# Four-layer graph network: when the second layer turns its attention weights, adds its elu and takes the next moments

## The chip, the core and the metric

The kernel runs on one core of a Trainium2 chip. The metric is the device time of one execution in microseconds, 724.43 as the median of three. The engines are TensorE (PE, with its weight loads listed as PEld), VectorE (DVE), ScalarE (ACT), GpSimd (POOL) and SyncE (SP). Each runs its own list of instructions in order; between engines, semaphores are counted up (`then_inc`) and waited for (`wait_ge`).

## What is computed

64 graphs of 128 nodes and 256 features pass four layers. Each layer normalises, applies relu, computes and adds its result to x:

```python
h = jnp.maximum(_layernorm(x), 0.0); x = x + L0(h)   # relations
h = jnp.maximum(_layernorm(x), 0.0); x = x + L1(h)   # attention with leaky relu, below
h = jnp.maximum(_layernorm(x), 0.0); x = x + L2(h)   # normalised adjacency
h = jnp.maximum(_layernorm(x), 0.0); x = x + L3(h)   # attention with 8 heads

# L1, the second layer
h = jnp.einsum('bnc,cf->bnf', x, W)
s1 = jnp.einsum('bnf,f->bn', h, a1); s2 = jnp.einsum('bnf,f->bn', h, a2)
e = jax.nn.leaky_relu(s1[:, :, None] + s2[:, None, :], negative_slope=0.2) * mask
att = jax.nn.softmax(e, axis=2)
out = jax.nn.elu(jnp.einsum('bij,bjf->bif', att, h) + beta * h)
```

## The kernel before

x stays in SBUF for all layers (`xs`). The work goes by pairs of graphs, 32 of them (`PAIRS`), and a layer is a software pipeline over the pairs: in step p each engine works on several pairs, each at a different stage. Everything is written out in Python; the order on each engine is the order of the code.

In step p of the second layer **PE** runs `product(p)` (L385, the features times W), `turn_prob(p - 3)` (L848, transposes the attention weights of pair p - 3 into bank 3), `turn(p + 1)` (L166, transposes the next normalised input), `attend(p - 3)` (L835, weights attT times values) and `spread(p)` (L873, one score as a row). The banks for attend are three, so attend(q) waits until elu(q - 3) has read its bank (`l1_x_done`).

**ACT** runs `copy_pT(p - 3)` (L912, the turned weights to attT), `copy_h(p)` (L907), `copy_hT(p + 1)` (L916), `softmax_exp(p - 1)` (L922), and for elu of pair p - 4 `elu_negative` (L929) and `elu_exp` (L935). `normalise_early(q)` (L282) are the first inputs of the third layer; number 0 stands after step 29, the others behind the loop.

**DVE** runs `scores(p - 1)` in step p: masked (L1019), inverse, leaky (L1026), `attention(p - 2)` (L1041, the weights), `elu(p - 6)` (L853, adds the positive part from the bank to x), maximum (L1031). Behind it stand the moments of odd pairs of this layer (L361, one graph in an odd step; in an even step the other, and then L366, L143 and L144 for nmean and vare), and in 16 steps, `UNIT_STEPS`, half a unit of the third layer's first moments (`moments_two`: L252, and at every second half L257). They are steps 8 to 26 without 12, 17 and 22. Behind the units of pairs 3 and 7 follow the arguments for the roots (L263, L264).

**POOL** in step p: every other step a root for an odd pair (L155), in steps 22 and 28 `root_two` (L270, L272, eight roots of the third layer); then it waits until attention(p - 2) is done, runs `add(p - 5)` (L987, the exponential part of elu onto x) and `centre_first(p + 2)` (L331, the normalised input). `add_bias_two` (L307) belongs to the third layer.

Behind the loop, the **tail** mixes the last pairs of the second layer with the first of the third: `gather` (L375), `outputs` (L395), `gathered_high` (L290) and `gathered_low` (L295), `update_two` (L301).

Of the kernel before, what the change touches and what calls it, by code (L numbers as in the profile page):

```python
# [9 lines left out]
ALU = mybir.AluOpType  # L10
# [4 lines left out]
def gnn_stack_kernel(nc, x, adj, w):  # L15
# [3 lines left out]
    PAIRS = GRAPHS // 2  # L19
# [10 lines left out]
    with ExitStack() as ctx:  # L30
# [215 lines left out]
        def moments_two(dve, q, g):  # L246
# [6 lines left out]
            if g == 1:  # L253
                ins.then_inc(l2_step, 1)
                dve.wait_ge(l2_step, 2 * q + 1)
                for g in range(2):
                    ins = nc.vector.bn_aggr(mv_two[:, q, g, :], stats_two[:, g, :])  # L257
                ins.then_inc(l2_step, 1)
                if q % 4 == 3:
                    dve.wait_ge(l2_step, 2 * q + 2)  # L260
                    mean, var = (mv_two[:, q - 3:q + 1, :, i].rearrange("p k g -> p (k g)") for i in range(2))
                    part = slice(2 * q - 6, 2 * q + 2)
                    nc.vector.scalar_tensor_tensor(nmean_two[:, part], mean, -2.0, mean, ALU.mult, ALU.add)  # L263
                    nc.vector.scalar_tensor_tensor(vare_two[:, part], var, EPS, var, ALU.add, ALU.max).then_inc(l2_two_stats, 1)  # L264
# [164 lines left out]
        with nc.Block() as block:  # L429
# [427 lines left out]
            def _(pe):  # L857
# [19 lines left out]
                def step(p):  # L877
                    product(p)
                    if p >= 3:
                        turn_prob(p - 3)  # L880
# [6 lines left out]
                    spread(p)  # L887

# [11 lines left out]
                turn_prob(PAIRS - 3)  # L900

            @block.scalar
            def _(act):
# [32 lines left out]

                def step(p):
# [7 lines left out]
                    if p >= 4:  # L945
                        elu_negative(p - 4)
                        elu_exp(p - 4)

                def elu_parts(p):
                    elu_negative(p)  # L950
                    elu_exp(p)
# [13 lines left out]
                elu_parts(PAIRS - 5)  # L965
# [18 lines left out]
            def _(pool):  # L984
# [4 lines left out]
                for p in range(PAIRS):  # L989
# [8 lines left out]
                    if p >= 5:  # L998
                        add(p - 5)
                    if p + 2 < PAIRS:  # L1000
                        centre_first(pool, p + 2, tr_done, p + 1)
                for p in range(3):
                    add_bias_two(pool, p)
                add(PAIRS - 5)
                add_bias_two(pool, 3)
# [8 lines left out]
            def _(dve):  # L1014
# [30 lines left out]
                def scores(p):  # L1045
# [6 lines left out]
                    if p >= 5:  # L1052
                        elu(p - 5)
                    maximum(p)

                def step(p):
# [9 lines left out]
                    if p in UNIT_STEPS:  # L1066
                        unit = UNIT_STEPS.index(p)
                        moments_two(dve, unit // 2, unit % 2)

                UNIT_STEPS = [p for p in range(8, 27) if p % 5 != 2]  # L1070
# [7 lines left out]
                elu(PAIRS - 6)  # L1078
# [4 lines left out]
                elu(PAIRS - 5)  # L1083
# [552 lines left out]
```

## Time and profile before

| | before |
|---|---|
| median of 3 runs | 724.43 us (724.25 to 724.78) |
| the profiled execution | 724.73 us, span 722.7 us |
| PE busy | 699.0 us (97%) |
| DVE busy | 623.9 us (86%) |
| ACT busy | 554.1 us (77%) |
| POOL busy | 461.7 us (64%) |
| chain of waits: PE, DVE, ACT | 87%, 6%, 3% |

The profile is of one execution; its time stands beside the span of its instructions. Starts are counted from the span's start. A row of the timeline gives start, duration, engine and line of the source, what is written and read, and in brackets how long the engine had been idle and who released it. The modelled end of a PE row reaches into the next, so PE is read by starts. The second layer's loop lies between about 180 and 300 us. PE's granted clock is 1.00 in every stretch of it.

### The profile page before, as it was taken

To read this page: it belongs to the slowest core of one execution; us is meant where nothing else is said; L and a number is where in the kernel's file an instruction comes from. 1 tells how busy PE (TensorE), PEld (TensorE's weight loads), DVE (VectorE), ACT (ScalarE), POOL (GpSimd) and SP (SyncE) were. 2 spreads that over 40 slices of the span, in tenths; PEclk is the share of its full clock that TensorE was granted. 3 is DMA by queue.
4 is the path that set the end of the run, shared out by engine and by line. 5 is a ranking of instruction groups with operands and counts; after the bars stand their busy time and mean duration, and the time that the engine had idled before them with its cause. 6 is when DMAs were issued, how large, how long until landed. Compare 5 with 4: busy or idle time off the path is not lost.

```text
span 722.7 us, 22547 instructions
## 1 busy us (share of the span) xinstructions
PE 699.0 (97%) x6938; PEld 655.3 (91%) x6938; DVE 623.9 (86%) x2618; ACT 554.1 (77%) x1892; POOL 461.7 (64%) x585
## 2 busy tenths in 40 slices
PE   6999999999999999999998999999999999999996
PEld 5999999998788787889998899999999999999995
DVE  5898988886789998689998998989988998988865
ACT  3666565655688888976664988899888988898895
POOL 2455545464477677678884767766677667766762
PEclk9999999999999999999999999999999999999999
DMA  7223300000000000000000000000000000000001
GB/s 243 84 84 98 88 29 0 0 0 1 0 1 2 1 2 0 2 1 1 0 0 1 17 18 31 29 29 15 29 29 29 27 18 29 29 29 16 31 32 44
DMA packets 21710, 20.30 MB, mean 28 GB/s; under 512 B 2449, under 2 KB 21649, under 8 KB 21649
## 3 DMA queue, kind: packets, MB, share of 16 engines
q1 hardware_dynamic: 19456, 18.16, 8.0%
q10 hardware_dynamic: 2192, 1.44, 0.7%
q8 instruction: 24, 0.39, 0.2%
q14 instruction: 38, 0.30, 0.2%
HBM read 11.21 MB, written 8.39 MB: 27 GB/s over the span
## 4 chain that ended last, share of the span: by engine, by line
PE 87%; DVE 6%; ACT 3%; issue 2%; DMA 1%; POOL 0%; ACTq 0%; DVEq 0%
PE bank L395 43%; PE bank L1278 8%; PE bank L385 5%; PE bank L166 5%; PE bank L1264 5%; PE bank L1288 4%; PE bank L478 4%; PE bank L835 4%; PE bank L425 3%; PE bank L375 3%; DVE xs L853 1%; PE bank L459 1%; DVE att L1041 1%; ACT prob L1374 1%; PE bank L873 1%
## 5 line engine op out<-in xcount | busy, mean ns | idle before, releaser
L1374 ACT ACTIVATE prob<-wide,small 128x128 f32<-128x128 f32 x504 | 195.7, 396 | 2.1 <-DVE small L1486 2.1
L1449 POOL TENSOR_TENSOR prob<-prob,small 128x512 f32<-128x512 f32 x127 | 132.2, 1042 | 100.1 <-DVE small L1500 98.1
L1486 DVE CUSTOM_DVE_ANT_0 wide<-bank,mbias 128x128 f32<-128x128 f32 x512 | 115.2, 285 | 0.1
L1374 ACT ACTIVATION_READ_ACCUMULATOR prob<-wide,small 128x1 f32 x504 | 97.9, 194 | 0.0
L155 POOL TENSOR_TENSOR rstd<-vare,mhalf 128x2 f32<-128x2 f32 x104 | 73.6, 708 | 19.8 <-DVE vare L144 19.6
L1278 PE MATMUL bank<-ident,prob 128*128 128x128 f32 x512 | 72.8, 275 | 3.5 <-POOL prob L1449 3.2
L634 POOL TENSOR_TENSOR rnorm<-norm,mhalf 128x2 f32<-128x2 f32 x32 | 22.3, 695 | 81.3 <-ACT relsq L575 81.3
L129 DVE BATCH_NORM_STATS2 stats<-xs 128x6 f32<-128x256 f32 (+1 forms) x176 | 65.5, 413 | 5.4 <-DMA xs<-in_x_dram 4.5
L239 POOL TENSOR_SCALAR xn<-xs,nmean,rstd 128x256 f32<-128x256 f32 x120 | 65.4, 554 | 5.5 <-POOL rstd L155 5.5
L1394 ACT COPY probT<-bank 128x512 f32<-128x512 f32 x96 | 52.4, 580 | 19.6 <-PE bank L1278 19.6
L1278 PEld LDWEIGHTS bank<-ident,prob 128*128 128x128 f32 x512 | 59.0, 141 | 4.9 <-POOL prob L1449 4.8
L385 PE MATMUL bank<-w,hT 128*128 128x258 f32 x256 | 61.4, 382 | 1.3 <-DVE oTs L741 1.1
L987 POOL TENSOR_TENSOR xs<-xs,exp_u 128x512 f32<-128x512 f32 x32 | 40.8, 1276 | 30.2 <-DVE att L1041 28.0
L166 PE MATMUL bank<-ident,xn 128*128 128x128 f32 x376 | 56.4, 272 | 0.0
L395 PE MATMUL bank<-w,yTs 128*128 128x256 f32 x384 | 53.4, 288 | 2.2 <-DVE xs L301 2.1
L395 PE MATMUL bank<-hTs,wq 128*128 128x256 f32 x384 | 54.3, 290 | 0.6 <-DVE hTs L1504 0.6
L395 PE MATMUL bank<-hTs,wk 128*128 128x256 f32 x384 | 53.7, 288 | 0.0
L395 PE MATMUL bank<-wv,hTs 128*128 128x256 f32 x384 | 53.5, 288 | 0.0
L385 PEld LDWEIGHTS bank<-w,hT 128*128 128x128 f32 x256 | 46.1, 190 | 7.4 <-issue 1.3
L395 PE MATMUL bank<-wo,oTs 128*128 128x256 f32 x384 | 51.4, 284 | 1.0 <-DVE oTs L1538 0.5
L395 PEld LDWEIGHTS bank<-hTs,wq 128*128 128x128 f32 x384 | 47.6, 188 | 4.4 <-DVE hTs L1504 0.8
L395 PEld LDWEIGHTS bank<-w,yTs 128*128 128x128 f32 x384 | 47.5, 189 | 4.4 <-DVE yTs L295 2.4
(168 smaller groups left out, 1930.9 us busy)
## 6 DMA issues: line engine op xcount, KB each, us to landing
out_dram<-xs SPq DMA_DIRECT2D x31, 256.0 KB, 2.1
xs<-in_x_dram SPq DMA_DIRECT2D x29, 256.0 KB, 2.7
xs<-in_x_dram ACTq DMA_DIRECT2D x1, 512.0 KB, 7.2
xs<-in_x_dram ACTq DMA_DIRECT2D x1, 256.0 KB, 3.8
wq<-in_L_gnn_Wq_dram SPq DMA_DIRECT2D x1, 256.0 KB, 3.4
wk<-in_L_gnn_Wk_dram ACTq DMA_DIRECT2D x1, 256.0 KB, 4.7
wv<-in_L_gnn_Wv_dram SPq DMA_DIRECT2D x1, 256.0 KB, 5.3
w<-in_L_gnn_W_dram SPq DMA_DIRECT2D x1, 256.0 KB, 7.0
```

Source lines behind the costliest of these rows:

```text
L129: ins = nc.vector.bn_stats(stats[:, b, g, :], x_of(p, g))
L155: nc.gpsimd.tensor_tensor(rstd[:, b, :], vare[:, b, :], mhalf[:, 0:2], ALU.pow).then_inc(rstd_ready, 1)
L166: ins = nc.tensor.transpose(pe_ps[:, c * 2 * N + g * N:c * 2 * N + (g + 1) * N], src[:, g, c * 128:(c + 1) * 128], ident[:, :])
L239: ins = nc.gpsimd.tensor_scalar(xnb[b][:, g, :], x_of(p, g), nmean[:, b, g:g + 1], rstd[:, b, g:g + 1], ALU.add, ALU.mult)
L385: ins = nc.tensor.matmul(ps_g, hT[:, c, g, :], weight[:, c, :], start=(c == 0), stop=(c == C - 1))
L395: ins = nc.tensor.matmul(ps, lhsT(a, c), rhs(b, c), start=(n == 0), stop=(n == len(terms) - 1))
L987: nc.gpsimd.tensor_tensor(x_pair(p), x_pair(p), exp_u[p % 2][:, :, :], ALU.add).then_inc(added, 1)
L1278: ins = nc.tensor.transpose(PT[r % 2][:, i * N:(i + 1) * N], prob[:, r, i, :], ident[:, :])
L1374: ins = nc.scalar.activation(prob[:, r, i, :], wide[:, r, i, :], ACT.Exp, bias=nmax[r][:, i:i + 1], scale=-1.0, accum_out=rsum[r][:, i:i + 1])
L1394: nc.scalar.copy(prob_turned[b][r], PT[r % 2][:, :].rearrange("p (i n) -> p i n", n=N)).then_inc(pt_ready, 1)
L1449: nc.gpsimd.tensor_tensor(prob[:, r, :, :], prob[:, r, :, :], rinv[r].unsqueeze(2).to_broadcast([128, QUAD, N]), ALU.mult).then_inc(prob_r ...
L1486: nc.vector.tensor_tensor_reduce(out=wide[:, r, i, :], in0=SS[r][:, i * N:(i + 1) * N], in1=mbias[:, :], scale=-1.0, scalar=3e38, op0=ALU. ...
```

## The change

The turn of a pair's attention weights moves to the end of the step in which DVE makes them: `turn_prob(p - 2)` as PE's last operation of step p, instead of `turn_prob(p - 3)` behind the product. Elu moves up by one step on ACT (pair p - 3 in step p), POOL (`add(p - 4)`) and DVE (`elu(p - 5)` in step p). The tail loses the pieces that moved into the loop. The third layer's moments stand in steps 8 to 15 and 18 to 25, and the arguments of the roots are an own function, in steps 17 and 27.

```diff
+        def root_arguments_two(dve, k):
+            dve.wait_ge(l2_step, 8 * k + 8)
+            mean, var = (mv_two[:, 4 * k:4 * k + 4, :, i].rearrange("p k g -> p (k g)") for i in range(2))
+            part = slice(8 * k, 8 * k + 8)
+            nc.vector.scalar_tensor_tensor(nmean_two[:, part], mean, -2.0, mean, ALU.mult, ALU.add)
+            nc.vector.scalar_tensor_tensor(vare_two[:, part], var, EPS, var, ALU.add, ALU.max).then_inc(l2_two_stats, 1)
...
                 def step(p):
                     product(p)
-                    if p >= 3:
-                        turn_prob(p - 3)
                     if p + 1 < PAIRS:
                         turn(p + 1)
...
                     if p >= 3:
                         attend(p - 3)
                     spread(p)
+                    if p >= 2:
+                        turn_prob(p - 2)
...
                 gather_nodes(pe, bank[1], 1, xn2, l2_xn_ready).then_inc(l2_yt_done, 1)
-                turn_prob(PAIRS - 3)
...
                     if p >= 1:
                         softmax_exp(p - 1)
-                    if p >= 4:
-                        elu_negative(p - 4)
-                        elu_exp(p - 4)
+                    if p >= 3:
+                        elu_parts(p - 3)
...
                 normalise_early(act, 2)
-                elu_parts(PAIRS - 5)
                 softmax_exp(PAIRS - 1)
...
-                    if p >= 5:
-                        add(p - 5)
+                    if p >= 4:
+                        add(p - 4)
...
-                    if p >= 5:
-                        elu(p - 5)
+                    if p >= 4:
+                        elu(p - 4)
...
+                    elif p in (17, 27):
+                        root_arguments_two(dve, p // 10 - 1)
-                UNIT_STEPS = [p for p in range(8, 27) if p % 5 != 2]
+                UNIT_STEPS = [*range(8, 16), *range(18, 26)]
```

PE, steps 30 and 31 and the end of the loop, before (`att0` and `att1` are the two buffers of the weights, `val` the values, `nadjT` the adjacency for the third layer):

```order
L385 MATMUL bank<-w1,hT 128x258 x4
L848 MATMUL bank<-ident,att1 128x128 x2
L166 MATMUL bank<-ident,xn2 128x128 x4
L835 MATMUL bank<-val3,attT 128x256 x2
L873 MATMUL bank<-ident,val2 128x128 x2
L385 MATMUL bank<-w1,hT 128x258 x4
L848 MATMUL bank<-ident,att0 128x128 x2
L375 MATMUL bank<-nadjT,xn 128x128 x4
L835 MATMUL bank<-val0,attT 128x256 x2
L873 MATMUL bank<-ident,val3 128x128 x2
L375 MATMUL bank<-nadjT,xn2 128x128 x4
L848 MATMUL bank<-ident,att1 128x128 x2
```

The same place after (its lines are numbered higher by two):

```order
L387 MATMUL bank<-w1,hT 128x258 x4
L166 MATMUL bank<-ident,xn2 128x128 x4
L837 MATMUL bank<-val3,attT 128x256 x2
L875 MATMUL bank<-ident,val2 128x128 x2
L850 MATMUL bank<-ident,att0 128x128 x2
L387 MATMUL bank<-w1,hT 128x258 x4
L377 MATMUL bank<-nadjT,xn 128x128 x4
L837 MATMUL bank<-val0,attT 128x256 x2
L875 MATMUL bank<-ident,val3 128x128 x2
L850 MATMUL bank<-ident,att1 128x128 x2
L377 MATMUL bank<-nadjT,xn2 128x128 x4
```

The turn of `att0`, which stood between the product and attend of step 31, now ends step 30, and that of `att1` ends step 31 ahead of the second gather.

ACT behind the loop, before (`xn2`, `xn`: early normalisations 1 and 2; `yTs`: gathered, high part):

```order
L907 COPY val3<-bank 128x516
L282 ACTIVATE xn2<-xs,shift_two,rstd_two 128x256 x2
L290 CAST yTs00<-bank 128x512
L922 ACTIVATE exp_e0,small<-leaky_e0,small 128x128 x2
L912 COPY attT<-bank 128x256
L290 CAST yTs10<-bank 128x512
L282 ACTIVATE xn<-xs,shift_two,rstd_two 128x256 x2
L929 ACTIVATE neg_u<-bank 128x512
L935 ACTIVATE exp_u1<-neg_u 128x512
L922 ACTIVATE exp_e1,small<-leaky_e1,small 128x128 x2
```

And after:

```order
L908 COPY val3<-bank 128x516
L284 ACTIVATE xn2<-xs,shift_two,rstd_two 128x256 x2
L292 CAST yTs00<-bank 128x512
L923 ACTIVATE exp_e0,small<-leaky_e0,small 128x128 x2
L913 COPY attT<-bank 128x256
L292 CAST yTs10<-bank 128x512
L284 ACTIVATE xn<-xs,shift_two,rstd_two 128x256 x2
L923 ACTIVATE exp_e1,small<-leaky_e1,small 128x128 x2
L913 COPY attT<-bank 128x256
```

The two elu operations ahead of the last pair's exponentials are gone from here.

DVE in step 14, before, from the weights of pair 12 on:

```order
L1041 SCALAR_TENSOR_TENSOR att0<-exp_e0,small,beta_ident 128x128 x2
L853 SCALAR_TENSOR_TENSOR xs<-bank,xs 128x512
L1031 TENSOR_REDUCE small<-leaky_e1 128x2
L361 BN_STATS stats<-xs 128x6
L366 BN_AGGR mv<-stats 128x2 x2
L143 SCALAR_TENSOR_TENSOR nmean<-mv 128x2
L144 SCALAR_TENSOR_TENSOR vare<-mv 128x2
L252 BN_STATS stats_two<-xs 128x6
L257 BN_AGGR mv_two<-stats_two 128x2 x2
```

In step 13, after, from the weights of pair 11 on:

```order
L1038 SCALAR_TENSOR_TENSOR att1<-exp_e1,small,beta_ident 128x128 x2
L855 SCALAR_TENSOR_TENSOR xs<-bank,xs 128x512
L1028 TENSOR_REDUCE small<-leaky_e0 128x2
L363 BN_STATS stats<-xs 128x6
L252 BN_STATS stats_two<-xs 128x6
L257 BN_AGGR mv_two<-stats_two 128x2 x2
```

Before, the heavier half of a unit came now in an even step, behind the longer half of the odd moments, now in an odd one; after, it always stands in an odd step.

## Rows read from the trace of the kernel before

**Rows 1.** Timeline: PE in steps 3 and 31; start, duration (us), engine, line, operation.

```profile
187.84 1.61 PEld L385 LDWEIGHTS bank<-w,hT 128*128 128x128 f32 x8 [0.31 <-ACT hT L916]
...
295.61 1.91 PE L385 MATMUL bank<-w,hT 128*128 128x258 f32 x8
```

**Rows 2.** Busy time by engine in five steps of the second layer.

```profile
245.60:264.50 18.90, 18.78 (x101) 15.40 (x101) 17.74 (x65) 15.68 (x44) 14.50 (x19) 1.00 0.00 1
```

**Rows 3.** Timeline: one step's PE operations, with two of ACT's in it.

```profile
249.20 1.91 PE L385 MATMUL bank<-w,hT 128*128 128x258 f32 x8
...
250.95 0.38 PE L848 MATMUL bank<-ident,att 128*128 128x128 f32 x2
...
251.17 0.60 PE L166 MATMUL bank<-ident,xn 128*128 128x128 f32 x4
...
251.37 0.37 ACT L912 COPY attT<-bank 128x256 f32<-128x256 f32 x1 [0.51 <-PE bank L848]
...
251.79 0.73 PEld L835 LDWEIGHTS bank<-val,attT 128*128 128x128 f32 x4 [0.26 <-ACT attT L912]
...
252.76 0.38 PE L873 MATMUL bank<-ident,val 128*128 128x128 f32 x2
...
252.98 1.91 PE L385 MATMUL bank<-w,hT 128*128 128x258 f32 x8
...
253.38 0.60 ACT L929 ACTIVATE neg_u<-bank 128x512 f32<-128x512 f32 x1
```

**Rows 4.** Table of waits: who waited for whom, us in total, times, longest.

```profile
PEld bank L835 <- ACT attT L912: 9.3, 28, 0.8
...
PE bank L835 <- DVE xs L853: 1.9, 5, 0.6
```

**Rows 5.** Timeline: PE, an attend whose weights were ready, and what follows.

```profile
298.47 1.03 PE L835 MATMUL bank<-val,attT 128*128 128x256 f32 x4
...
299.34 0.38 PE L873 MATMUL bank<-ident,val 128*128 128x128 f32 x2
```

**Rows 6.** Timeline: DVE, the end of one step and the steps before and after 249.45.

```profile
233.28 0.41 DVE L252 BATCH_NORM_STATS2 stats_two<-xs 128x6 f32<-128x256 f32 x1
...
233.89 0.58 DVE L1019 SCALAR_TENSOR_TENSOR masked_e<-bank,val,adj_sb 128x128 f32<-128x128 f32 x2
...
245.63 0.61 DVE L1019 SCALAR_TENSOR_TENSOR masked_e<-bank,val,adj_sb 128x128 f32<-128x128 f32 x2 [0.85 <-PE bank L873]
...
249.45 0.59 DVE L1019 SCALAR_TENSOR_TENSOR masked_e<-bank,val,adj_sb 128x128 f32<-128x128 f32 x2
...
250.07 0.42 DVE L1026 SCALAR_TENSOR_TENSOR leaky_e<-masked_e 128x256 f32<-128x256 f32 x1
...
251.87 0.42 DVE L361 BATCH_NORM_STATS2 stats<-xs 128x6 f32<-128x256 f32 x1
...
252.20 0.41 DVE L252 BATCH_NORM_STATS2 stats_two<-xs 128x6 f32<-128x256 f32 x1
```

**Rows 7.** Timeline: POOL's add and centre in that step, and its early root.

```profile
251.10 1.27 POOL L987 TENSOR_TENSOR xs<-xs,exp_u 128x512 f32<-128x512 f32 x1 [0.78 <-DVE att L1041]
...
252.36 1.10 POOL L331 TENSOR_SCALAR xn<-xs,nmean,rstd 128x256 f32<-128x256 f32 x2
...
260.97 1.65 POOL L270 TENSOR_TENSOR rstd_two<-vare_two,mhalf 128x8 f32<-128x8 f32 x1
```

**Rows 8.** Timeline: one operation of POOL and one of DVE in the tail.

```profile
316.86 1.28 POOL L987 TENSOR_TENSOR xs<-xs,exp_u 128x512 f32<-128x512 f32 x1 [1.32 <-ACT exp_u L935]
...
317.00 1.16 DVE L143 SCALAR_TENSOR_TENSOR nmean<-mv 128x2 f32<-128x2 f32 x1
```

**Rows 9.** Timeline: PE's product of step 30, ACT's early normalisation.

```profile
291.48 1.91 PE L385 MATMUL bank<-w,hT 128*128 128x258 f32 x8
...
293.04 1.08 ACT L282 ACTIVATE xn<-xs,shift_two,rstd_two 128x256 f32<-128x256 f32 x2
```

**Rows 10.** Timeline: PE, the outputs of pair 7 in the third layer.

```profile
323.58 1.68 PE L395 MATMUL bank<-w,yTs 128*128 128x256 f32 x12
```

More of the change, by code:

```diff
@@ L258, in moments_two @@
                 ins.then_inc(l2_step, 1)
[L259 to L264, printed above, removed]
+        def root_arguments_two(dve, k):
[4 more added lines that the diff above has]
+            nc.vector.scalar_tensor_tensor(vare_two[:, part], var, EPS, var, ALU.add, ALU.max).then_inc(l2_two_stats, 1)
         def root_two(pool, k):
@@ L935, in elu_exp, with elu_parts @@
                     nc.scalar.activation(exp_u[p % 2][:, :, :], neg_u[:, :, :], ACT.Exp, scale=-1.0).then_inc(eu_ready, 1)
+                def elu_parts(p):
+                    elu_negative(p)
+                    elu_exp(p)
                 def step(p):
@@ L944, in step @@
                         softmax_exp(p - 1)
-                    if p >= 4:
-                        elu_negative(p - 4)
-                        elu_exp(p - 4)
-                def elu_parts(p):
-                    elu_negative(p)
-                    elu_exp(p)
+                    if p >= 3:
+                        elu_parts(p - 3)
                 for p in range(PAIRS - 1):
@@ L997, in _ @@
                         pool.wait_ge(prob_ready, p - 1)
-                    if p >= 5:
-                        add(p - 5)
+                    if p >= 4:
+                        add(p - 4)
                     if p + 2 < PAIRS:
                         centre_first(pool, p + 2, tr_done, p + 1)
-                for p in range(3):
+                for p in range(4):
                     add_bias_two(pool, p)
-                add(PAIRS - 5)
-                add_bias_two(pool, 3)
                 add(PAIRS - 4)
@@ L1077, in _ @@
                 attention(PAIRS - 2)
-                elu(PAIRS - 6)
+                elu(PAIRS - 5)
                 maximum(PAIRS - 1)
@@ L1082, in _ @@
                 attention(PAIRS - 1)
-                elu(PAIRS - 5)
                 update_two(dve, 0, 0)
```

## The prediction

> **What bounds the kernel now.** I read the busy time by stretches first, then the step starts in the timeline, then the table of waits, then single steps on each engine. TensorE (PE) is busy nearly throughout, so a change can pay only where PE waits or where one of its instructions takes longer than it must. The second layer is such a place. Its step p = 3 begins at 187.84 and its step 31 at 295.61 [rows 1]: 107.77 us for 28 steps, 3.85 each. In five steps without disturbance (245.60 to 264.50) each engine has, per step of 3.78: PE 3.76, VectorE (DVE) 3.55, ScalarE (ACT) 3.14, GpSimd (POOL) 2.90 [rows 2]. PE looks full there, but it isn't at its own rate. One step reads, by starts [rows 3]: product 249.20 to 250.95 (1.75), turn of the weights to 251.17 (0.22), turn of the next input, whose four transposes are twice two and so 0.44, attend at 251.79, spread at 252.76, next product at 252.98 (0.22). Attend's weight load stood idle for 0.26 until ACT had copied attT. The table of waits has this 28 times, 9.3 us in all, and beside it 1.9 us in which attend waited for elu on DVE (xs L853) [rows 4]. An attend whose attT was there long before takes 0.87 from its start to the next instruction [rows 5]. So a step without a wait costs 1.75 + 0.22 + 0.44 + 0.87 + 0.22 = 3.50 us, and PE now pays 3.78 and more.
>
> **The turn of the weights.** It moves from behind the product of step q + 3 to the end of step q + 2. Between it and attend(q) lay the 0.44 us of one turn, in which ACT had to see it, copy it (it begins at 251.37, after an idle 0.51 [rows 3]) and tell PE; now the product lies there as well, 2.19 us in all. What it waits for is attention(q), which DVE ends about 1.6 us into step q + 2, while its new place is 3.28 into that step: no wait until DVE is 1.6 late. The number of instructions is unchanged. Removed per step: 3.78 - 3.50 = 0.28, the 0.26 of the weight load [rows 3] and rounding. The product, now right behind it, waits for hT; ACT no longer sits waiting for the turned weights before it copies val and hT, so it makes hT earlier, and I cost this at nothing.
>
> **Elu one step up.** attend(q) needs elu(q - 3) done, for the bank. That elu was in the same step's DVE work, just before attend; it is now one step earlier, so the 1.9 us of [rows 4] go. ACT's two elu operations for p - 3 now wait for an attend of the same step; attend ends about 3.2 into the step, ACT came to the first of them at 253.38, 4.18 after the product's start, and comes the 0.5 us earlier in which it sat idle before attT [rows 3], so at about 3.7. POOL's add(p - 4) needs the exponential of the step before, which ends about 1.4 into the step; POOL starts the add at 1.65, released by attention [rows 6, 7]. Both are nothing while these covers of 0.5 and 0.3 us last, and each costs what exceeds them. ACT's own work, 3.14 per step, leaves 0.36 of 3.50.
>
> **What is late next: DVE with POOL.** The moments of the third layer now lie in steps 8 to 15 and 18 to 25 with no gap. An even step of that kind holds the full odd moments and half a unit: 249.45 - 245.63 = 3.82. An odd one holds 251.87 - 249.45 = 2.42 for the scores and elu, 252.20 - 251.87 = 0.33 for half of the odd moments, and 233.89 - 233.28 = 0.61 for the heavy half of a unit: 3.36 [rows 6]. Steps without a unit are 0.33 shorter at even p (3.49) and take 2.75 at odd p; the root arguments that now stand in steps 17 and 27 (two small operations) fall into such short steps. But DVE can't always go as fast as that. POOL's add holds DVE's nmean: begun at 317.00 under an add that began at 316.86 and lasts 1.28, it takes 1.16 instead of 0.15 to 0.3, and ends 0.02 after the add [rows 8]. leaky and attention read two SBUF operands like it. In the loop of before nothing of POOL lies on them, since the add waits for attention, and add and centre are over 252.36 + 1.10 - 249.45 = 4.01 us after DVE began the step, while the next leaky comes 0.62 into the following one [rows 6, 7]. At a shorter period they touch: a DVE step is then not under 4.01 - 0.62 = 3.39. The Trainium skill, page "SBUF — State Buffer", section "Who interferes with whom", says that a DVE instruction with two SBUF inputs and a GpSimd instruction that reads SBUF exclude each other for a whole instruction, the later one blocking; the stretched nmean agrees, and by that rule the same floor follows. If the row stood only for nmean's own small form and leaky and attention ran freely, the floor would fall away, and the demand below would be 1.5 less.
>
> DVE's demand from step 8 to 27 is then 8 x (3.82 + 3.39) + 2 x (3.49 + 3.39) = 71.4 us against PE's 20 x 3.50 = 70.0: 1.4 late. POOL's root for eight values, 1.65 [rows 7] and with the shift behind it about 1.89, stays in steps 22 and 28 and pushes the end of add and centre to 0.62 + 1.89 + 1.26 + 1.10 = 4.87; leaky is then held by 4.87 - (3.82 + 0.62) = 0.4 and, in the shorter step 28, by 4.87 - (3.49 + 0.62) = 0.8. That makes 2.6 us late in all. How late may DVE be before PE waits? The maximum comes 2.42 into a DVE step; behind it ACT runs exponentials, two elu operations and the copy of attT, some 2.2 us (3.14 less about 0.95 for the copies of val and hT, an estimate), and attend needs this at 3.50 + 2.19 = 5.69. That is about 1.0 us of room, so PE loses 2.6 - 1.0 = 1.6. The bounds: nothing, if lag is absorbed or the floor isn't there; and 4.4, if POOL's later operations hold leaky for another 0.28 (a quarter of centre's 1.10) in each of these ten odd steps. I take 1.6, since the 3.82 and 3.36 are measured and only the room is an estimate.
>
> **Step 30.** ACT's first early normalisation (293.04, two of them 1.08 long [rows 9]) lies between two steps; it made step 30 last 295.61 - 291.48 = 4.13 [rows 1, 9]. It adds about 1.03 to ACT's 3.14 and now meets a shorter period: 3.14 + 1.03 - 3.50 = 0.67, so step 30 is 4.17. What was won by the early turn is given back in this one step.
>
> **The tail** runs from step 31 to the product of pair 7 in the third layer at 323.58 [rows 10], 27.97 us. ACT loses one pair's two elu operations there, each about as long as the 0.60 of [rows 3], so the exponentials of pair 31 can come some 1.1 earlier. But ACT later waits again for the turn of pair 31, whose place in PE's order is unchanged, and PE comes to it only as much earlier as its own waits shrink: attend(29) no longer waits for elu (0.25), and the low half for pair 0 is 0.2 earlier. I take 0.5; bounds 0 and 1.1. POOL's lock on nmean at 317.00 can shift either way, 0.6 at most by my estimate. The third layer's own loop behind it is PE's and doesn't change.
>
> **Sum.** 27 x 3.50 + 4.17 + 1.6 = 100.3 against 107.77: 7.5 saved, with the tail 8.0. The start (steps 0 to 2) is a chain through ACT and gains nothing: the first turn fits in PE's wait for hT, 0.31 at 187.84 [rows 1]. The profiled execution took 724.73 around its span of 722.7, and 0.3 more than the median of the three runs (724.43). 724.73 - 8.0 = 716.7; on the median, 716.4.
>
> **Rivals.** (1) The lag is hidden whole: no floor, or more room. 107.77 - 98.7 = 9.1, with the tail 9.6 (10.2 at its bound): 714.8, at best 714.2. For it: room of 1.0 has cover in ACT's slack; against: DVE had 3.55 of work per step, which is over 3.50. (2) DVE and POOL set the pace: POOL holds leaky a quarter of centre more in every odd step, PE loses 4.4. 107.77 - 98.7 - 4.4 + 0.5 = 5.2: 719.2. For it: the shift of POOL against DVE is new, and centre ends just where leaky begins. (3) Attend gets no faster, because the weight load is slow for another reason than the wait; then only the waits for elu go, 107.77 - 28 x 3.78 = 1.9: 722.5. Against: [rows 5]. (4) Slower: POOL comes to lie on leaky with its whole centre (1.1) or add in every step, because it never catches up. DVE's mean step (3.82 + 3.36) / 2 = 3.59 would be 4.1 or more; it decides from 3.85 - 3.59 = 0.26 of holding per step. At 0.55 (one of centre's two instructions) it gives 28 x (4.14 - 3.85) = 8.1 us lost: 732.5. Against it: the add waits for attention, which sets POOL right again in each step, and POOL has 2.90 of work in 3.78.
>
> **How the numbers follow.** The forecast, 716.4, has 0.50; rival 1 0.20; rival 2 0.17; rival 3 0.07, and half-effects near no change another 0.02; rival 4 0.04. The range leaves out rivals 3 and 4 and part of 2, and takes in rival 1 with the tail's bound: 714.0 to 719.4. A measurement of this kernel can tell about 0.2% (1.4 us) from no change. Faster by more than that are forecast, rivals 1 to 3: 0.94; same 0.02; slower 0.04.
>
> **What would show it.** In the profile after: the wait of attend for attT gone from the table (below 1 us), step starts of the product 3.50 apart in steps 4 to 8, elu before attend no longer a releaser; in steps 8 to 27 DVE with no idle before masked, leaky at times above 0.42, and PE's waits some 1.6 us in sum with ACT's attT or POOL's xn as releaser, most of them from step 19 on; step 30 as long as before; PE's last waits of the tail still there. If steps are 3.78 apart, rival 3 holds; if leaky is long in every odd step, rival 2. The prediction is wrong if PE's own instructions change their time in the new order.

## The result and the profile after

The changed kernel takes **716.56 us** (716.39 to 717.35, four runs) against 724.61 us (724.25 to 725.30) of the kernel before on the same chip: a ratio of 0.9889, interval 0.9877 to 0.9901. The forecast was 716.4 in a range of 714.0 to 719.4. The profiled execution took 716.58 with a span of 714.8, 7.9 less than the 722.7 of before. The sum is right; where the 7.9 lie is not all as forecast:

| part of the span, by starts of PE operations | before | after | saved | forecast |
|---|---|---|---|---|
| start to product of step 3 | 187.84 | 188.58 | -0.74 | 0 |
| step 3 to step 31 | 107.77 | 101.05 | 6.72 | 7.5 |
| step 31 to outputs of pair 7 | 27.97 | 27.31 | 0.66 | 0.5 |
| from there to the end | 399.12 | 397.86 | 1.26 | 0 |

Loop and tail, the parts that the change touches, saved 7.4 where 8.0 was forecast. The other two rows nearly cancel. Most of the gain at the end is not the change's doing; where the loss at the start comes from is known only in part. Both are looked at below.

The page after, busy time by engine. Each engine has as many instructions as before. DVE is busy 4.0 us longer all the same, 1.4 of it in leaky, which takes 471 ns on average instead of 428: an operation that is held up counts as busy.

```profile
PE 692.3 (97%) x6938; PEld 652.9 (91%) x6938; DVE 627.9 (88%) x2618; ACT 555.9 (78%) x1892; POOL 462.1 (65%) x585
```

The table of waits after (who waited <- for whom: us, times, longest), to be held against [rows 4]:

```profile
PEld bank L837 <- ACT attT L913: 2.3, 8, 1.1
...
PE bank L837 <- ACT attT L913: 0.9, 1, 0.9
...
PEld bank L166 <- POOL xn L333: 1.5, 4, 0.5
```

28 waits of the weight load for attT have become eight, 9.3 us have become 2.3; the row of 0.9 is the matmul behind the longest of them, in step 30, and so the same wait once more. Attend's waits for elu (1.9) are gone. A new wait is there, of the turn of the next input for POOL's centre.

Busy time by engine in steps 8 to 16 (PE, PEld, DVE, ACT, POOL, then the granted clock), against [rows 2]:

```profile
206.46:235.09 28.63, 28.63 (x161) 24.39 (x161) 28.19 (x102) 26.17 (x72) 23.20 (x29) 1.00 0.00 1
```

DVE, 17.74 of 18.90 us before, is now busy for 28.19 of 28.63. That alone doesn't show that it sets the pace (units_light below does). The PE operations of steps 11 and 12 say how (start, duration, engine, line, operation; in brackets idle time and releaser):

```profile
217.14 1.91 PE L387 MATMUL bank<-w,hT 128*128 128x258 f32 x8
218.88 0.60 PE L166 MATMUL bank<-ident,xn 128*128 128x128 f32 x4
219.32 1.03 PE L837 MATMUL bank<-val,attT 128*128 128x256 f32 x4
220.19 0.38 PE L875 MATMUL bank<-ident,val 128*128 128x128 f32 x2
220.40 0.38 PE L850 MATMUL bank<-ident,att 128*128 128x128 f32 x2
220.62 1.91 PE L387 MATMUL bank<-w,hT 128*128 128x258 f32 x8
...
224.29 0.38 PE L387 MATMUL bank<-w,hT 128*128 128x258 f32 x1
```

Step 11 is 220.62 - 217.14 = 3.48, made up as the forecast said: 1.74 + 0.44 + 0.87 + 0.21 + 0.22. Step 12 is 3.67, since attend's weights came late there:

```profile
222.89 0.73 PEld L837 LDWEIGHTS bank<-val,attT 128*128 128x128 f32 x4 [0.16 <-ACT attT L913]
```

DVE's masked operations of three steps in a row, from the same stretch:

```profile
218.02 0.59 DVE L1016 SCALAR_TENSOR_TENSOR masked_e<-bank,val,adj_sb 128x128 f32<-128x128 f32 x2
...
221.38 0.58 DVE L1016 SCALAR_TENSOR_TENSOR masked_e<-bank,val,adj_sb 128x128 f32<-128x128 f32 x2
...
225.18 0.59 DVE L1016 SCALAR_TENSOR_TENSOR masked_e<-bank,val,adj_sb 128x128 f32<-128x128 f32 x2
```

3.36 and 3.80 us: 7.16 for a pair of steps, where PE itself wants 6.97. I call the distance from a product's start to the masked operation of that step DVE's lag: 218.02 - 217.14 = 0.88 in step 11. PE waits for nothing in step 11 itself. But ACT makes attT for step 12 behind the exponentials of step 11, so a lag is to be read against the length of the step that follows it: step 12, with its late weights.

**How far PE was from its own rate.** Step lengths after, less PE's own 3.487:

| steps | 3 | 4 to 6 | 7 | 8 | 9 to 16 | 17 to 21 | 22 to 26 | 27, 28 | 29 | 30 |
|---|---|---|---|---|---|---|---|---|---|---|
| excess, us in all | 0.10 | 0 | 0.18 | 0 | 0.93 | 0 | 0.78 | 0 | 0.30 | 1.13 |

That is 3.4 us; the forecast had 1.6 for DVE's lateness and 0.67 in step 30.

**Step 30** shows the largest single loss. POOL has its second root of eight values (L272) in step 28, and the timeline of POOL, DVE, ACT and PE behind it reads:

```profile
278.77 1.80 POOL L272 TENSOR_TENSOR rstd_two<-vare_two,mhalf 128x8 f32<-128x8 f32 x1
...
280.81 1.27 POOL L986 TENSOR_TENSOR xs<-xs,exp_u 128x512 f32<-128x512 f32 x1
281.17 0.93 DVE L143 SCALAR_TENSOR_TENSOR nmean<-mv 128x2 f32<-128x2 f32 x1
...
282.73 0.70 DVE L1023 SCALAR_TENSOR_TENSOR leaky_e<-masked_e 128x256 f32<-128x256 f32 x1
283.21 0.42 PEld L166 LDWEIGHTS bank<-ident,xn 128*128 128x128 f32 x4 [0.49 <-POOL xn L333]
...
284.92 0.40 ACT L923 ACTIVATE exp_e<-leaky_e,small 128x128 f32<-128x128 f32 x1 [0.41 <-DVE small L1028]
...
286.84 1.08 ACT L284 ACTIVATE xn<-xs,shift_two,rstd_two 128x256 f32<-128x256 f32 x2
287.83 0.35 ACT L913 COPY attT<-bank 128x256 f32<-128x256 f32 x1
288.23 1.13 PE L837 MATMUL bank<-val,attT 128*128 128x256 f32 x4 [0.88 <-ACT attT L913]
```

The late add holds DVE's nmean (0.93 instead of 0.15 to 0.3) and the late centre its leaky (0.70 instead of 0.43). By that DVE's maximum is late for ACT's exponentials (idle 0.41), and the turn of pair 30's input waits for xn. So ACT comes late to its normalisation, which stands ahead of the copy of attT. Step 30 took 289.63 - 285.01 = 4.62 us; it was 4.13 before.

**The start.** The 0.74 is there far ahead of anything that the change moved. The same operation of the first layer, before and after:

```profile
20.73 0.96 PE L425 MATMUL bank<-oTs,rels 128*128 128x256 f32 x6
```

```profile
21.49 0.96 PE L427 MATMUL bank<-oTs,rels 128*128 128x256 f32 x6
```

A late transfer has a part in it. DVE's first operation, before and after:

```profile
4.50 0.75 DVE L129 BATCH_NORM_STATS2 stats<-xs 128x6 f32<-128x256 f32 x2 [4.50 <-DMA xs<-in_x_dram]
```

```profile
5.01 0.75 DVE L129 BATCH_NORM_STATS2 stats<-xs 128x6 f32<-128x256 f32 x2 [5.01 <-DMA xs<-in_x_dram]
```

PE's first product starts 0.51 later with it. In a second profile of the changed kernel (after_again below) the transfer is in time (4.49), and yet that operation of the first layer starts at 21.25, and step 3 at 188.38. There PE's first operations take longer, at a granted clock of 1.00 in both: the first eight matmuls 3.78 instead of 3.52, the four turns behind them 1.06 instead of 0.60. In the profiles of the kernels below step 3 begins between 187.8 and 188.6. The first product takes 3.49 in units_only, the only one of them with neither turn nor elu moved, and 3.78 in all the others. So the start varies by 0.2 with one and the same kernel, and a slower first stretch of PE is in every profile of a kernel with turn or elu moved and in neither of the two without. With one or two profiles of each this can be the program's doing or not; it is open. The lengths of loop and tail don't contain it.

**The end.** Of the 1.26, 1.0 is one product near the end of the fourth layer. It starts 10.7 us before the span's end. Before, the PE row of the timeline, and then busy time by engine in four stretches (the granted clock is the third number from the end):

```profile
712.00 2.64 PE L395 MATMUL bank<-wo,oTs 128*128 128x256 f32 x12 [0.47 <-DVE oTs L1509]
```

```profile
705.00:710.00 5.00, 3.20 (x49) 2.81 (x50) 4.36 (x34) 5.00 (x21) 1.95 (x3) 1.00 0.00 0
710.00:712.00 2.00, 1.19 (x9) 0.74 (x9) 1.44 (x3) 2.00 (x8) 0.81 (x1) 1.00 0.39 131
712.00:714.80 2.80, 2.80 (x14) 2.80 (x15) 2.34 (x6) 0.37 (x1) 1.04 (x1) 0.55 0.02 6
714.80:722.70 7.90, 4.06 (x52) 3.35 (x50) 2.26 (x5) 1.91 (x4) 0.00 (x0) 0.93 0.20 66
```

After:

```profile
705.17 1.64 PE L397 MATMUL bank<-wo,oTs 128*128 128x256 f32 x12 [0.47 <-DVE oTs L1507]
```

PE had been busy for 3.20 of 5.00 and 1.19 of 2.00 us, and then was granted 0.50, the level of 1.2 GHz, from 712.3 to 715.7, and 1.00 again from 716 on. It comes and goes with one and the same kernel. The changed kernel's runs have spans of 714.6 to 714.8 at a mean clock of 1.00 and 715.6 at 0.997; in its second set 713.9 (twice) against 715.2 to 715.3. The kernel before has both too, 721.7 to 722.2 and 722.4 to 723.0 beside that second set. So about 1 us of the profiled difference is not the change's, and the loss at the start hid it. Not every such difference is the clock's: one run of units_light has a span of 713.4 at a mean clock of 1.00, the others 712.0 to 712.2. Medians mix such runs, which limits what they can tell between the kernels below to about 1 us.

### The profile page after: what moved, and what is told of

It is laid out like the page before. It is cut to its first block, busy times and chain, and to the rows that moved or that the text cites. A ratio compares the mean times of both kernels' runs of the same rounds, so it can differ in the third digit from the quotient of the medians.

```text
span 714.8 us, 22548 instructions
## 1 busy us (share of the span) xinstructions
PE 692.3 (97%) x6938; PEld 652.9 (91%) x6938; DVE 627.9 (88%) x2618; ACT 555.9 (78%) x1892; POOL 462.1 (65%) x585
## 4 chain that ended last, share of the span: by engine, by line
PE 89%; DVE 3%; ACT 3%; issue 2%; POOL 1%; DMA 1%; POOLq 0%; ACTq 0%; DVEq 0%
PE bank L397 43%; PE bank L1276 8%; PE bank L387 7%; PE bank L166 5%; PE bank L1262 5%; PE bank L1286 4%; PE bank L480 4%; PE bank L837 3%; PE bank L427 3%; PE bank L377 3%; PE bank L461 1%; PE bank L875 1%; PE bank L850 1%; ACT prob L1372 1%; DMA wk<-in_L_gnn_Wk_dram 1%
```

## The experiments

My theory: PE's step falls to 3.5, because the turned weights are there in time; what PE doesn't get, DVE's work in the steps with moments and ACT's normalisation in step 30 take. The rivals for the gain: that it comes from one part alone, or from the moments' new places. The rivals for the loss: that it isn't DVE but ACT or PE's own instructions. Each kernel ran beside the kernel before on its chip, whose medians there were 724.12 (turn_only to old_units), 724.13 (units_light to norm_in_30) and 724.20 (the last four), so medians of different groups are compared by their ratios. "Loop" is step 3 to 31, "tail" step 31 to the outputs of pair 7.

| kernel | median, us | ratio (interval) | loop | tail |
|---|---|---|---|---|
| before | 724.61 | | 107.77 | 27.97 |
| changed | 716.56 | 0.9889 (0.9877 to 0.9901) | 101.05 | 27.31 |
| turn_only | 721.92 | 0.9969 (0.9957 to 0.9982) | 106.00 | 27.62 |
| elu_only | 721.60 | 0.9968 (0.9954 to 0.9982) | 106.18 | 27.50 |
| units_only | 722.43 | 0.9976 (0.9966 to 0.9986) | 106.28 | 27.98 |
| old_units | 717.51 | 0.9908 (0.9892 to 0.9925) | 102.05 | 27.28 |
| units_light | 713.96 | 0.9864 (0.9847 to 0.9880) | 98.71 | 27.29 |
| even_in_3 | 716.00 | 0.9881 (0.9864 to 0.9897) | 100.03 | 27.30 |
| root_in_30 | 714.97 | 0.9871 (0.9855 to 0.9888) | 99.89 | 27.30 |
| norm_in_30 | 715.63 | 0.9886 (0.9869 to 0.9902) | 99.69 | 27.86 |
| after_again | 716.99 | 0.9891 (0.9876 to 0.9906) | 100.79 | 27.28 |
| three_moves | 714.91 | 0.9866 (0.9850 to 0.9883) | 98.56 | 27.87 |
| split_root | 714.54 | 0.9871 (0.9854 to 0.9887) | 98.14 | 27.87 |
| split_swap | 714.24 | 0.9864 (0.9847 to 0.9880) | 98.29 | 27.27 |

### One part alone

**turn_only**: the kernel before with only the turn moved.

```diff
                     product(p)
-                    if p >= 3:
-                        turn_prob(p - 3)
...
                     spread(p)
+                    if p >= 2:
+                        turn_prob(p - 2)
...
-                turn_prob(PAIRS - 3)
```

> The kernel before with only the turn of the weights moved to the end of the step; elu and the moments stay. Theory (attend's weight load no longer waits for attT, but attend still waits for elu of its own DVE step, which ends 2.2 us into the step when DVE is on time): PE has no room for DVE's lag, so each step lasts as long as DVE's work in it where that is over 3.49 (even steps with half a unit 3.8, steps with heavy work on both sides 4.1 to 4.4). About 4 to 5 us are saved, 719.5 to 720.5, and the wait of attend for elu grows from 1.9 us to several. Rival (the turn is worth its 0.26 in every step alone): 717. Rival (only both together give anything): 724.

**elu_only**: the kernel before with only elu moved up, on ACT, POOL and DVE, and in the tail to match.

```diff
-                    if p >= 4:
-                        elu_negative(p - 4)
-                        elu_exp(p - 4)
+                    if p >= 3:
+                        elu_negative(p - 3)
+                        elu_exp(p - 3)
...
-                    if p >= 5:
-                        add(p - 5)
+                    if p >= 4:
+                        add(p - 4)
...
-                    if p >= 5:
-                        elu(p - 5)
+                    if p >= 4:
+                        elu(p - 4)
...
```

> The kernel before with only elu moved up by one step on ACT, POOL and DVE and in the tail. Theory: the waits of attend for elu (1.9 us in five steps) go, the waits for attT stay at 0.26 each, the tail gains at most 0.5: 722.1 to 722.8. Rival (the elu of the same step makes ACT late with attT): no gain or slower, 724.5 to 726.

**units_only**: the kernel before with only the new places of moments and root arguments.

```diff
...
+                    elif p in (17, 27):
+                        root_arguments_two(dve, p // 10 - 1)
...
-                UNIT_STEPS = [p for p in range(8, 27) if p % 5 != 2]
+                UNIT_STEPS = [*range(8, 16), *range(18, 26)]
```

> The kernel before with only the third layer's moments in steps 8 to 15 and 18 to 25 and their root arguments in steps 17 and 27. Theory: steps that were heavy on both sides (15, 17, 25 and 27, which took 3.98, 4.30, 3.99 and 4.30) fall to 3.78, so 1.4 to 1.6 us go: 723.0. Rival (the gapless stretch makes DVE late elsewhere): 724.4 or more.

**old_units**: the changed kernel with the old places, so turn and elu together.

```diff
...
-                    elif p in (17, 27):
-                        root_arguments_two(dve, p // 10 - 1)
...
-                UNIT_STEPS = [*range(8, 16), *range(18, 26)]
+                UNIT_STEPS = [p for p in range(8, 27) if p % 5 != 2]
```

> The changed kernel with the moments of the third layer back in their old steps (turn and elu as changed). Theory (PE takes up to 0.9 us of DVE's lag, beyond that it goes at DVE's pace, and DVE's work in sum is the same): 0.3 to 1 us slower than the changed kernel, 716.9 to 717.6, with the loss in steps 15 to 19 and 25 to 28. Rival (the spread of the moments carries much of the gain): 718 or more. Rival (it carries nothing): 716.5.

Each part alone is worth 1.5 to 1.8 us of the loop, the first two together 5.7, all three 6.7. I had expected more of the turn alone: 2.2 us in the medians, not 4 or so. Its table of waits says what stood in the way:

```profile
PE bank L835 <- DVE xs L853: 2.2, 5, 0.7
```

In turn_only, attT is there in time, but attend(p - 3) still needs the elu of the same step, which DVE finishes just before it. Its steps are 3.70 long with DVE hardly lagging, though the table names only five waits; the others show as idle times of 0.18 to 0.30 without a releaser ahead of attend's weight load:

```profile
250.72 0.73 PEld L835 LDWEIGHTS bank<-val,attT 128*128 128x128 f32 x4 [0.30 <-issue]
```

That it is elu can be read from the ends: in each of 24 steps of turn_only (6 to 29) the weight load starts 0.11 to 0.13 behind the end of DVE's elu, and attT had been there for 0.58 or more. So two waits of PE lay nearly side by side at one instruction, 0.28 and 0.2 long over a step of 3.49. Taking away either uncovers the other, and the steps with much DVE work become longer than before (17 and 27: 4.38 and 4.36 instead of 4.30). elu_only shows the other half. It takes only the five waits for elu; its steps stay at 3.77 to 3.78, with attT as the wait, but tolerate lags of up to 0.8:

```profile
PEld bank L835 <- ACT attT L912: 7.7, 28, 0.6
```

Its median, 721.60, is half a microsecond below the expected range; loop and tail gave 2.1, the rest lies outside them. units_only, with 722.43 half a microsecond better than expected, levels the heavy steps at 3.78 (step 17 and 27: 4.30 before) and changes nothing else, which is all that it could do while attT comes late. In old_units (717.51, in the expected 716.9 to 717.6) the two moves together leave DVE's uneven load as the limit: lags up to 1.32, and steps 18 and 28 of 4.12 and 4.11. There the new places are worth 102.05 - 101.05 = 1.0, or 1.3 against the second profile of the changed kernel.

### Is it DVE's load that PE waits for?

**units_light**: the changed kernel, its third-layer moments over a quarter of the features.

```diff
-            ins = nc.vector.bn_stats(stats_two[:, g, :], x_of(q, g))
+            ins = nc.vector.bn_stats(stats_two[:, g, :], x_of(q, g)[:, 0:64])
```

> The changed kernel with the first moments of the third layer taken over 64 of the 256 features (so the third layer's first norms are only near). DVE has about 0.25 us less in each of 16 steps. Theory (in the changed kernel PE goes at DVE's pace, 7.15 per two steps, as soon as DVE's lag has used up the room of 0.9 us): the waits of attend in steps 9 to 16 and 24 to 26 go, those around the roots in steps 22 to 24 get smaller, steps are 3.49 there; 1.0 to 1.5 us less than the changed kernel, 715.0 to 715.6. Rival (not DVE's work but POOL's hold on leaky sets the pace, a DVE step is never under 3.39): 0.3 less at most. Rival (PE's own rate): no change.

It is: steps 9 to 28 fall to 3.48 or 3.49 but for one of 3.62, and the loop to 98.71. The same instructions are there, on PE, ACT and POOL with the same work. DVE's busy share doesn't tell the two kernels apart: in the stretch shown above it is 28.22 of 28.63 us here. It gave more than expected, 713.96 where 715.0 to 715.6 was, since steps 29 and 30 gained too, 3.49 and 4.37, where I had counted on the middle alone. The rival of a DVE step that is never under 3.39 is out: odd steps with a unit were 3.16 long, though leaky began 0.22 before the end of POOL's centre; it took 0.50 instead of 0.43.

**even_in_3**: in the changed kernel, the last moments of the even pairs (L342 to L354) in step 3 instead of 5.

```diff
-                        if p == 5:
+                        if p == 3:
                             moments_even(dve, PAIRS // 2 - 1)
```

> The changed kernel with the last even pairs' moments (two statistics, two aggregates and two small operations, 1.2 us of DVE) in step 3 instead of step 5. Theory (they bring DVE's lag to 0.88 in step 6, before the units begin, and DVE is idle 1.6 us in step 3): the lag at step 8 is near 0, PE's waits of 0.2 in steps 7, 9, 10 and 12 go and later ones remain; 0.5 to 0.8 us less than the changed kernel, 715.8. Rival (the lag comes back from the units within two steps): no change, 716.5.

Before the change these 1.2 us hid in step 5's cover. After it DVE's lag is -0.01 in step 5 and 0.88 in step 6. DVE makes this up in the steps without moments and is on time again in step 8 (-0.01), but POOL isn't. Its add of step 7, released by DVE's weights, is late, its centre then lies on leaky (0.74 instead of 0.43), and its root for the even pairs, of eight values (L316), runs to 209.28, so that the next add lies on nmean (0.65):

```profile
207.04 0.74 DVE L1023 SCALAR_TENSOR_TENSOR leaky_e<-masked_e 128x256 f32<-128x256 f32 x1
207.47 1.81 POOL L316 TENSOR_TENSOR rstd_even<-vare_even,mhalf 128x8 f32<-128x8 f32 x1
...
209.24 1.27 POOL L986 TENSOR_TENSOR xs<-xs,exp_u 128x512 f32<-128x512 f32 x1
...
209.88 0.65 DVE L143 SCALAR_TENSOR_TENSOR nmean<-mv 128x2 f32<-128x2 f32 x1
```

DVE's step 8 lasts 4.58, and it is 1.08 late in step 9, so that the stretch with moments begins with its room used up; in even_in_3 these are 3.75 and 0.25. In step 3 there is still idle time: steps 7 to 15 are then 3.48 to 3.49, and the loop 100.03 (changed kernel: 101.05 and 100.79). The 0.8 to 1.0 are smaller in the medians, 716.00 against 716.56 and 716.99 on other chips, half of its runs having the low clock at the end.

### Step 30

**root_in_30**: POOL's second root of eight values in step 30.

```diff
-                    if p in (22, 28):
-                        root_two(pool, (p - 22) // 6)
+                    if p in (22, 30):
+                        root_two(pool, (p - 22) // 8)
```

> The changed kernel with POOL's second early root of eight values in step 30 instead of 28. Theory (in step 28 it pushes add and centre onto DVE's nmean, 0.93 instead of 0.33, and leaky, 0.70 instead of 0.42, and the input of pair 30 comes late for PE's turn, 0.3): step 29 falls from 3.79 to 3.5 and step 30 from 4.62 to about 4.3; 0.5 to 0.7 us less than the changed kernel, 715.9. Rival (step 30 is set by ACT's normalisation alone): 0.3 less. Rival (the root is now late for the tail, since add of pair 26 stands behind it): no change or slower, 716.5 to 717.5.

**norm_in_30**: ACT's first early normalisation in step 30 behind the copy of hT, no longer ahead of the copy of attT.

```diff
                         copy_hT(p + 1)
+                    if p == PAIRS - 2:
+                        normalise_early(act, 0)
...
                     step(p)
-                    if p == PAIRS - 3:
-                        normalise_early(act, 0)
```

> The changed kernel with ACT's early normalisation 0 in step 30 behind the copy of hT, ahead of the exponentials, instead of between steps 29 and 30. Theory (it stands in front of the copies of attT, val and hT, so attend of pair 27 waits 0.9): step 30 falls from 4.62 to 3.5 to 3.7, up to 0.5 comes back in step 31, where attend of pair 28 waits for its copy behind the gather; 0.6 to 1.0 us less, 715.7. Rival (ACT's work is the same, the whole is given back in the tail, which ACT sets): no change, 716.5.

Both theories of the loss in step 30 hold, each for its part. Without the root in step 28, add and centre come in time (the same place in root_in_30: nmean 0.33 long instead of 0.93, leaky 0.43 instead of 0.70):

```profile
279.11 1.28 POOL L986 TENSOR_TENSOR xs<-xs,exp_u 128x512 f32<-128x512 f32 x1 [0.88 <-DVE att L1038]
...
280.60 0.33 DVE L143 SCALAR_TENSOR_TENSOR nmean<-mv 128x2 f32<-128x2 f32 x1
...
281.55 0.43 DVE L1023 SCALAR_TENSOR_TENSOR leaky_e<-masked_e 128x256 f32<-128x256 f32 x1
```

Step 29 is 3.49 and step 30 4.15, just the 4.17 that the forecast had from ACT's work alone, and ACT's exponentials no longer wait for DVE there. With the normalisation moved and the root left, step 30 is 3.65, but the tail grows by 0.55: the exponentials of pair 29 and what follows them in the tail come a normalisation later. Of 1.36 won in the loop 0.8 remain. In both kernels 0.4 of what the loop won against the changed kernel's first profile lies in steps 7 to 10 and is not of the edit (see the nmean of the even pairs in the last section); against its second, 100.79, the loop won 0.90 and 1.10. root_in_30's median, 714.97, is 0.9 below what I expected, norm_in_30's as expected.

### A version that beats both

**after_again** is the changed kernel once more, beside the next three on one chip; **three_moves** has the edits of even_in_3, root_in_30 and norm_in_30 together.

> The changed kernel unchanged, beside the next three. Both theories: 716.0 to 716.6. It also tells whether the wait of POOL's add and centre on DVE's small operation in step 5 (0.54 in one trace of this kernel, 0.17 in traces of kernels with the same code there) comes and goes between runs, and whether the last product of the fourth layer runs at the full clock.

> The changed kernel with the even moments in step 3, POOL's second root in step 30 and ACT's normalisation 0 in step 30 behind the copy of hT. Theory (each removes a different wait of PE in the loop: 0.3 to 0.5 before step 16, 0.3 in step 29, 1.1 in step 30, and 0.5 comes back in the tail, which ACT sets): loop from step 3 to 31 98.6 to 98.9 instead of 101.0, time 1.7 to 2.2 less than the changed kernel, 714.0 to 714.5. Rival (they take away the same wait, the chain through ACT around step 30): 715.3.

**split_root**: three_moves with the roots of eight in two halves, the first one's in steps 18 and 20, the second one's both in step 30.

```diff
+                    if p in (18, 20):
+                        half_root_two(pool, 0, (p - 18) // 2)
+                    if p == 20:
+                        shift_two_of(pool, 0)
+                    if p == 30:
+                        half_root_two(pool, 1, 0)
+                        half_root_two(pool, 1, 1)
+                        shift_two_of(pool, 1)
```

> As the one before, and POOL's first root of eight values in two halves of four, in steps 18 and 20, where the values have been there since step 17. Theory (in step 22 the whole root of 1.65 pushes centre behind PE's turn and onto leaky; one half costs about 1.0 and ends before leaky): steps 22 to 24 fall from 3.60, 3.77 and 3.70 to 3.49 to 3.55, 0.4 to 0.6 less than the one before. Rival (DVE's lag from the units holds PE there anyway): 0.1 to 0.2 less.

**split_swap**: split_root with two of DVE's elu operations in the tail ahead of the root arguments of the third layer.

```diff
                     update_two(dve, p - 2, b)
+                    if between is not None:
+                        elu(between)
                     if norms:
                         root_argument(dve, p + 3, dstep, stats_ready, 1 - b)
```

> As the one before, and in the tail DVE's elu of pairs 30 and 31 stands ahead of the root arguments of the third layer instead of behind them. Theory (nmean is held 1.08 by POOL's add there; elu, with one operand in PSUM, isn't, so it can run meanwhile): the tail from step 31 to the outputs of pair 7 is 0.4 to 0.6 shorter. Rival (the elu is held as well, or ACT sets the tail): no change.

The loop falls from 100.79 to 98.56 in three_moves and 98.14 in split_root, where 28 steps at PE's own rate would be 97.6: nothing much is left there. after_again's median, 716.99, is above the expected 716.0 to 716.6: three of its five runs have a mean clock of 0.997 or 0.998, the other two take 715.66. three_moves is as expected in the loop; its median, 714.91, lies between the 714.5 of the theory and the 715.3 of the rival. split_root brought steps 22 to 24 to 3.48, 3.49 and 3.63. split_swap gets the tail's 0.6 back (27.27): an elu runs its usual 0.68 under POOL's add, and nmean behind it takes 0.57 where it took 1.16, though the outputs behind pair 7 come only 0.3 earlier, so half of it is lost again in the next. In the medians these are 716.99, 714.91, 714.54 and 714.24, the differences of the last three below what they can tell. split_swap beats the changed kernel by 2.75 us on one chip (ratios to before 0.9864 against 0.9891, though their intervals overlap between 0.9876 and 0.9880). In profiled spans it is 712.0 against 715.2, of which about 1 is the clock at the end, so loop and tail give 2.2 to 2.5.

## Why the prediction held, step by step

- **What bounds the kernel.** Right: an attend with its weights in time made a step of 3.48, forecast 3.50 from the pieces of [rows 3, 5]. Over 27 steps the difference is 0.35 in the change's favour. Rival 3 is out.
- **Turn and elu.** Their sum was right (units_light, where DVE is seldom late, saved 9.06 in the loop, where the forecast without lateness had 9.1), their split was not. I gave the 0.28 per step to the turn and 1.9 in all to elu; the runs give 1.8 and 1.6 alone and 5.7 together. The step that failed is "removed per step: 3.78 - 3.50 = 0.28" as the turn's own worth. The wait for elu was hidden behind the wait for attT: a releaser is named only for the wait that ends last.
- **The covers of the moved elu.** Right: on ACT and POOL it cost nothing in steps 4 to 6, which stand at PE's own rate.
- **DVE with POOL.** The pair of steps is 7.16, forecast 7.21 (3.82 and 3.39). The odd step was 3.36, DVE's own work in [rows 6], not POOL's floor of 3.39; this stretch can't tell the two apart. units_light can: with odd steps of 3.16 the floor was not where I put it. The lock itself was seen elsewhere, on nmean and leaky above. The Trainium skill's rule (page "SBUF — State Buffer", section "Who interferes with whom"), a lock for a whole instruction with the later one blocking, agrees: nmean ended at 282.10, POOL's add at 282.08.
- **The room.** 1.0 was an estimate, and 0.3 too much. Behind a step without a wait, a lag of 0.79 made the next step 0.10 longer, 0.82 made it 0.12, 0.88 made it 0.18, 1.03 made it 0.32 and 1.31 made it 0.62 (changed kernel, even_in_3 and old_units); lags up to 0.63 cost nothing. That is about 0.7 of room. A third of what is missing is in attend: with late weights it takes 0.97 to the next instruction instead of 0.87.
- **PE's loss outside step 30**: 101.05 - 27 x 3.487 - 4.62 = 2.3, forecast 1.6. Two terms were mis-sized. The room is one; with 0.7 the forecast's own 2.6 of lateness would have cost 1.9. The other is DVE's lateness in steps 8 and 9: I counted POOL's roots in steps 22 and 28 and not its root for the even pairs in step 8, which step 5's 1.2 us of moments (an operation that I had not read in the trace) made late. even_in_3 gave back 0.8 to 1.0, more than the missing 0.7. So of the signs in the profile two failed: attend's wait for attT is 2.3 and not below 1, and half of PE's loss outside step 30, 1.2, lies before step 17, not from step 19 on.
- **Step 30.** Forecast 4.17, measured 4.62. I took ACT's own work and the normalisation, 0.67 over PE's step, and did not carry on the lateness of 0.8 that I had myself worked out for the root in step 28. root_in_30 brought 4.15. This term is short by 0.45.
- **The tail**: 0.66 for 0.5. **Sum** of loop and tail: 0.7 and 0.45 more lost, 0.35 and 0.15 more gained, 7.4 instead of 8.0.
- **Start and end.** The forecast had nothing for either. The loss of 0.74 in the first 20 us and the gain of 1.26 behind the tail, 1.0 of it the clock, made up for the missing 0.6. That the median fell within 0.2 of the forecast was thus partly luck; its own error is 0.6.
- **Rivals.** Rival 2 (leaky long in every odd step) is out: leaky has 0.42 and 0.43 in steps 11 to 13. Rival 1 wanted 9.6 saved in loop and tail, where 7.4 came; only units_light, with less work on DVE, had it (9.06 and 0.68). Rival 4 did not happen: the add stayed behind attention.

## What to carry to other kernels

When two producers' waits end at one instruction, price both before costing the removal of either: the table names only the later, and here each removal alone gave under a third of the two together. In a software pipeline, carry a lag from step to step with its room, beginning at the first step of the loop; a burst that a slower loop hid (1.2 us in step 5, roots of 1.8 us in steps 8 and 28) takes the room that the next heavy steps need, and it can be handed on by an engine that is nowhere near busy all the time, here POOL. Read gains by stretches between marks on the bounding engine: with one and the same kernel the end of the span moved by about 1 us and its start by 0.2.

## What the runs showed of the hardware

- **TensorE's clock near the end.** From 10.4 to 7.0 us before the span's end of the kernel before, the clock was granted at 0.50, in some executions of a kernel and not in others; one product of 12 matmuls took 2.64 instead of 1.64. In the 7 us ahead of that product PE had been busy for 4.39 in the kernel before and in the changed kernel's second profile, where the clock fell, and for the same 4.39 in its first profile and in norm_in_30, where it didn't. So nothing in PE's own work tells the two apart. Runs of one kernel with a mean clock of 0.997 or 0.998 have spans mostly 0.5 to 1.4 us longer.
- **A small DVE operation slips in between two of POOL's, or doesn't.** The same nmean of the even pairs (128x8) under POOL's centre took 0.54 in one profile of the changed kernel and 0.17 in the second one (after_again):

```profile
199.15 0.54 DVE L353 SCALAR_TENSOR_TENSOR nmean_even<-mv_even 128x8 f32<-128x8 f32 x1
```

```profile
198.93 0.17 DVE L353 SCALAR_TENSOR_TENSOR nmean_even<-mv_even 128x8 f32<-128x8 f32 x1
```

  It started 0.58 behind the start of POOL's centre (two instructions, 1.09 together) in the one, 0.55 in the other, and 0.55 to 0.57 in the profiles of root_in_30, norm_in_30, units_light and old_units, all with 0.17. The lag in step 6 was 0.88 with the one and 0.51 with the others, and step 7 3.67 or 3.48. A few hundredths of a microsecond decide such a lock.
- **elu, with one operand in a bank, and POOL's add don't hold each other.** In turn_only (timeline of DVE and POOL) the add begins 0.16 into an elu; neither is longer than elsewhere (0.68 to 0.69, and 1.27 to 1.28), while nmean, with no operand from a bank, took 0.93 under such an add:

```profile
249.92 0.68 DVE L853 SCALAR_TENSOR_TENSOR xs<-bank,xs 128x512 f32<-128x512 f32 x1
...
250.08 1.28 POOL L986 TENSOR_TENSOR xs<-xs,exp_u 128x512 f32<-128x512 f32 x1 [0.78 <-DVE att L1040]
```
